# Value products issued two rounds at a time, and causal masks added by half-array matmuls, in an attention loop

## The reference

```python
H, D = 16, 8                                   # 16 heads of 8 columns
q, k, v = heads(x @ Wq + bq), heads(x @ Wk + bk), heads(x @ Wv + bv)
att = where(causal, q @ k.T * D**-0.5, -inf)   # 256 queries, 256 keys
y = softmax(att) @ v
qc, kc, vc = heads(x @ Wcq + bcq), heads(ctx @ Wck + bck), heads(ctx @ Wcv + bcv)
y = y + softmax(qc @ kc.T * D**-0.5) @ vc      # 256 queries, 512 context keys
x = x + tanh(g_xattn[0]) * (y @ Wp + bp)       # x is layer-normalised ahead of the products
```

## Time and profile before

| | us |
|---|---|
| timed runs, median (lowest to highest of 3) | 378.12 (374.95 to 379.81) |
| the profiled execution | 374.34 |
| its span, first to last instruction | 372.6 |
| TensorE busy (share of the span) | 326.8 (88%) |
| VectorE busy | 233.9 (63%) |
| ScalarE busy | 191.7 (51%) |
| mean granted clock of TensorE | 0.948 of full speed |

### The profile page before, as it was taken

The page is one execution under the profiler, slowest core; times in us unless marked ns, Lnnn a source line. Parts: engine busy times, 40 slices in busy tenths (PEclk is TensorE's granted clock), DMA queues, the critical chain, the costliest instruction groups (busy, mean ns, idle before and its releaser), DMA issues.

```text
span 372.6 us, 7109 instructions
## 1 busy us (share of the span) xinstructions
PE 326.8 (88%) x2696; PEld 188.9 (51%) x2696; DVE 233.9 (63%) x546; ACT 191.7 (51%) x397; POOL 110.0 (30%) x202
## 2 busy tenths in 40 slices
PE   4689799979999999789989799999987599899994
PEld 2446433424434344244476467677755266565662
DVE  5889998858888879466442143332213679649765
ACT  3267388858898888557248323322247143323220
POOL 5526231316433233123575003443350201100000
PEclk9999879989999999899989699999998599989999
DMA  7759792960323005230161560000004000000001
GB/s 177 172 124 210 132 195 56 213 187 4 115 74 102 4 2 173 73 102 3 26 214 35 128 184 10 18 23 21 10 21 118 0 0 3 0 0 2 28 1 28
DMA packets 35777, 27.80 MB, mean 75 GB/s; under 512 B 5579, under 2 KB 33022, under 8 KB 35744
## 3 DMA queue, kind: packets, MB, share of 16 engines
q1 hardware_dynamic: 33574, 25.27, 27.4%
q0 software_dynamic: 1280, 1.88, 1.6%
q10 hardware_dynamic: 890, 0.20, 0.3%
HBM read 11.89 MB, written 5.26 MB: 46 GB/s over the span
## 4 chain that ended last, share of the span: by engine, by line
PE 69%; DVE 13%; ACT 6%; DMA 4%; issue 4%; POOL 2%; ACTq 1%; SPq 0%; POOLq 0%; DVEq 0%
PE psum L1468 12%; PE psum L1672 11%; PE psum L1703 7%; PE psum L1691 4%; DVE nmax L1042 4%; PE psum L1434 4%; PE psum L1650 4%; PE psum L1410 3%; PE psum L1486 3%; PE psum L1402 3%; ACT ot_sb L818 2%; PE psum L1412 1%; PE psum L1655 1%; PE psum L1765 1%; PE psum L1437 1%
## 5 line engine op out<-in xcount | busy, mean ns | idle before, releaser
L1042 DVE TENSOR_REDUCE nmax<-psum 128x2 f32<-128x1024 f32 (+2 forms) x88 | 103.2, 1216 | 15.6 <-PE psum L1410 11.3
L843 ACT ACTIVATE parts<-psum 128x512 f32<-128x512 f32 (+1 forms) x88 | 44.7, 569 | 9.3 <-PE psum L1434 8.8
L1672 PE MATMUL psum<-p_more,kcat 128*128 128x320 f32 x128 | 42.6, 475 | 0.7 <-DVE p_more L1176 0.7
L1185 DVE TENSOR_TENSOR qcat<-psum,qk_r 128x320 f32<-128x320 f32 x32 | 15.7, 491 | 42.8 <-ACT qk_r L886 42.6
L733 POOL DMA_INDIRECT rows_back<-qcat,back_at x24 | 22.9, 953 | 53.1 <-ACT qcat L876 48.2
L886 ACT ACTIVATE qk_r<-psum 128x320 f32<-128x320 f32 x32 | 14.0, 437 | 45.2 <-PE psum L1672 45.2
L1703 PE MATMUL psum<-h_t,kcat 128*128 128x512 f32 x64 | 30.9, 608 | 0.7 <-ACT h_t L854 0.7
L1410 PE MATMUL psum<-kcat,qcat 64*128 64x512 bf16 x128 | 25.9, 404 | 5.5 <-DVE nmax L1042 4.8
L1672 PEld LDWEIGHTS psum<-p_more,kcat 128*128 128x128 f32 x128 | 23.4, 200 | 13.5 <-issue 4.6
L1468 PE MATMUL psum<-parts,v_aug 128*9 128x256 f32 (+1 forms) x352 | 28.9, 373 | 0.0
L1434 PE MATMUL psum<-qcat,kcat 64*128 64x256 bf16 x256 | 25.6, 280 | 3.0 <-ACT p_more L843 1.2
(11 more groups left out here) (225 smaller groups left out, 609.5 us busy)
## 6 DMA issues: line engine op xcount, KB each, us to landing
kcat<-parts SPq DMA_DIRECT2D x18, 192.0 KB, 4.1
qcat<-parts SPq DMA_DIRECT2D x24, 128.0 KB, 3.9
kcat<-ones_b SPq DMA_DIRECT2D x8, 192.0 KB, 5.2
kcat<-in_L_ffn_wi_gate_dram SPq DMA_DIRECT2D x6, 256.0 KB, 3.8
kcat<-in_L_ffn_wi_up_dram SPq DMA_DIRECT2D x6, 256.0 KB, 4.0
kcat<-in_L_ffn_wo_dram SPq DMA_DIRECT2D x6, 256.0 KB, 5.5
parts<-in_L_ffn_w_dram SPq DMA_DIRECT2D x3, 512.0 KB, 5.5
rows_in<-zeros SPq DMA_DIRECT2D x1, 1290.0 KB, 5.8
```

Of the source, the lines that this page charges most:

```text
L843: act.activation(p_slots[u % NPT][:, 0:w], s2_bank(s2_place[u])[:, 0:w], ACT.Exp, scale=SCALE).then_inc(p_in, 1)
L1042: dve.tensor_reduce(dst[:, :, n * g:n * (g + 1)], src.rearrange("p (r q k) -> p r q k", r=PAR, q=n), AX.X, ALU.max, negate=True).then_inc( ...
L1185: dve.tensor_tensor(hh[:, e % 2, f, 0:SLOTS], bank(3 + 2 * (i % 2))[:, 0:SLOTS], sg[:, i % 2, 0:SLOTS], ALU.mult).then_inc(hh_in[0], 1)
L1672: ins = pe.matmul(bank(2 + 2 * (i % 2) + m)[:, 0:SLOTS], w_t[e][:, m, f * P:(f + 1) * P], xs_t[:, e % 2, :], start=True, stop=True)
```

## The change

Two things. `ROUNDS_AT` puts rounds 2 and 3 of the values together behind step 3's scores, and rounds 4 and 5 behind step 5's; steps 2 and 4 then have none. And the mask of each tile is added by 64-row matmuls: head `par` 0's by the upper half of the array's rows, head `par` 1's by the lower half, each half in two turns (64 mask rows per turn, shifted by widened tiles `ident_w` and `mask_w`), alternating between the halves. A tile's mask takes two matmuls in place of one. `bv_wide` moves into the space of `got`.

```diff
-        bv_wide = sb("bv_wide", [P, D])
...
-        ident_b = sb("ident_b", [P, P], BF16)
-        mask_b = sb("mask_b", [P, P], BF16)
+        ident_w = sb("ident_w", [P, 2 * P], BF16)
+        mask_w = sb("mask_w", [P, 2 * P], BF16)
+        ident_b = ident_w[:, P // 2:P // 2 + P]
...
         got = sb("got", [P, 2, NT, D])
+        bv_wide = got[:, 0, 0, :]
...
-        ROUNDS_AT = ((), (0, 1), (2,), (3,), (4,), (5,))
+        ROUNDS_AT = ((), (0, 1), (), (2, 3), (), (4, 5))
...
+            link(pool.memset(ident_w[:, :], 0.0))
             const(pool.tensor_copy(ident_b[:, :], ident[:, :]))
-            link(pool.memset(mask_b[:, :], 0.0))
-            const(pool.affine_select(out=mask_b[:, :], in_=mask_b[:, :], pattern=[[-1, P]], compare_op=ALU.is_ge,
-                                     fill=NEG, base=0, channel_multiplier=1))
+            link(pool.memset(mask_w[:, :], 0.0))
+            const(pool.affine_select(out=mask_w[:, :], in_=mask_w[:, :], pattern=[[-1, 2 * P]],
+                                     compare_op=ALU.is_ge, fill=NEG, base=P // 2, channel_multiplier=1))
...
                 if kind != "cross":
-                    for par in range(PAR):
-                        dst, w = bank(first + par), BANK // heads
+                    w = BANK // heads
+                    for turn in range(2):
                         for n in range(heads):
-                            pe.matmul(dst[:, (n + 1) * w - P:(n + 1) * w], ident_b[:, :], mask_b[:, :],
-                                      start=(n == 0), stop=False, skip_group_check=True)
+                            for par in range(PAR):
+                                rows = slice(64 * par, 64 * par + 64)
+                                shift = slice(64 * (1 + par - turn), 64 * (1 + par - turn) + P)
+                                pe.matmul(bank(first + par)[:, (n + 1) * w - P:(n + 1) * w], ident_w[rows, shift],
+                                          mask_w[rows, shift], start=(turn == 0 and n == 0), stop=False,
+                                          skip_group_check=True)
```

## The result

The changed kernel takes 379.75 us (median of 20 runs, 377.5 to 384.47), the kernel before 377.88 in the same series (20 runs, 374.91 to 383.22). The ratio is 1.0049, interval 1.0025 to 1.0072: **slower by 1.9 us** (0.9 to 2.7). The forecast was +4.2 us, a ratio of 1.011. The sign is right and the range holds the time; the size is less than half of the forecast. The kernel before was timed again beside each of three groups of experiments, each on another chip (medians 374.18, 378.13 and 374.13 us); times are compared within a group only.

A forecast was written before the change was run, and what follows sets the result against it. TensorE was taken to bound the kernel, with waits on ScalarE's exps behind each step's scores. Terms 3.32 - 0.64 - 0.47 + 0.66 + 1.32 = +4.2 us on the 378.12 median gave 382.3 us, range 376 to 386.

The forecast's parts named there:

- the wait for the ring: Attention loop: a step's scores wait for the previous step's first exp on ScalarE (three banks); bare, 1.07 or 0.90 us.
- the first gap: TensorE idle 2.36 us at 78.05 for nmax_t copied into qcat; the clock's return there was priced at 0.
- groups 4 to 12: Loop's middle, six steps on four heads each: odd groups +3.32 us, even -0.64, group 12 -0.47.
- groups 13 to 15: Loop's last groups, without maxima: +0.66 us for two longer steps, +1.32 for round 4 coming behind the last step.
- The absorption of groups 1 to 3 in the transfer's wait: Before 78.05 these groups add 1.50 us, hidden in TensorE's 2.36 us wait for a transfer: counted 0.
- rival 1: Attention loop: only TensorE's work counts, the wait on ScalarE having slack; -4.8 us, 373.3; chance 0.10.
- rival 2: Attention loop: new idle makes TensorE's clock fall to 1.2 GHz; 21 us over half the groups, 403; chance 0.05.
- rival 3: Even groups: the 64-row masks don't run in pairs; +3.0 us over five groups, 385.3; chance 0.05.
- rival 4: At 78 and behind the 1.84 gap the clock may not fall, returning up to 1.0 each: 380.3; no separate chance.
- the short gaps: New TensorE idle of some 0.45 us, twice per odd group; the reason given for counting no return of the clock.
- The second gap: Group 12's end: TensorE waits 1.84 us for GpSimd's split of the last maxima; the clock's return was priced at 0.
- the loop's first group: 0: VectorE bounds this group, its maxima running 12.81 us without a gap, so the change adds 0.

The follow-up runs named there:

- experiment 5: Kernel before with part 2's maxima sent to qcat ahead of batch 3's layout in SP's queue: 374.25 against 378.13 us, ratio 0.9902.
- experiment 6: Changed kernel with part 2's maxima sent ahead of batch 3's layout in SP's queue: 379.21 us, ratio 1.0028 to the kernel before.
- experiment 2: Changed kernel with the old ROUNDS_AT, so only the masks are new against the kernel before: 372.33 us, ratio 0.9957.
- experiment 7: Kernel before, unchanged, executed once more for a second trace: 379.83 us.
- experiment 9: Kernel before with 8 unread matmuls ahead of the last turn's wait at 152 us alone: 372.23 us, ratio 0.9958.
- experiment 3: Changed kernel with the doubled rounds behind steps 2 and 4 in place of 3 and 5: 378.66 us, ratio 1.0127 to the kernel before.
- experiment 11: Kernel before with new masks, earlier transfer of part 2's maxima and 8 unread matmuls ahead of the last turn: 369.87 against 378.13 us, ratio 0.9789.
- experiment 10: Changed kernel, unaltered, run again: 375.22 us, ratio 1.0039 to the kernel before.
- experiment 8: Kernel before with 10 unread matmuls ahead of the wait at 78 us alone: 373.1 against 374.13 us, ratio 0.998.
- experiment 4: Kernel before with unread matmuls ahead of both long waits, 10 at 78 us and 8 at 152 us: 370.79 us, ratio 0.9919.

## Why the prediction was right in sign and wrong in size

The stretches of the profiled executions, in us, cut at the loop's first `scores2`, group 4's first, the last `turn`, the last `scores2`, and the experts' first matmul:

| kernel | to group 4 | to last turn | to last scores | to experts |
|---|---|---|---|---|
| before | 32.31 | 74.36 | 25.97 | 31.09 |
| before, once more | 32.96 | 74.57 | 26.16 | 35.55 |
| before, first gap filled | 32.19 | 73.41 | 26.14 | 30.45 |
| before, second filled | 32.17 | 74.39 | 24.68 | 31.21 |
| before, both filled | 32.39 | 73.31 | 24.68 | 31.26 |
| before, early transfer | 31.05 | 73.38 | 24.66 | 35.40 |
| masks alone | 31.58 | 73.11 | 24.65 | 31.32 |
| masks, early transfer, second filled | 29.71 | 71.70 | 24.68 | 34.87 |
| rounds alone | 32.52 | 76.18 | 27.15 | 31.82 |
| pairs behind the other steps | 31.92 | 77.25 | 25.08 | 31.11 |
| after | 31.57 | 75.53 | 27.04 | 33.53 |
| after, once more | 31.63 | 75.56 | 27.24 | 31.36 |
| after, early transfer | 31.74 | 75.56 | 28.31 | 33.68 |

**Right: the wait for the ring, and its size.** Between group 4 and the last turn the change costs 75.55 - 73.36 = +2.2 (two traces each) against the kernel before with its clock kept up behind the first gap; the forecast for groups 4 to 12 was 3.32 - 0.64 - 0.47 = +2.2. From the last turn to the last scores it costs 27.04 - 0.75 (the new fall: 2.00 for 1.25) - 24.68 = +1.6, and the weight transposes behind start another 0.44 later; forecast +1.98 for groups 13 to 15, found 2.0. The absorption of groups 1 to 3 in the transfer's wait is right too, and experiments 5 and 6 show its price when that wait is gone, 1.54.

**Refuted: rivals 1, 2 and 3.** TensorE's work fell by 7 us and the time rose; the middle groups keep 1.00 (but group 15, below, does not); the masks run in pairs.

**Wrong, the step: rival 4, "I take neither, because the short gaps ahead of both remain".** The clock's return behind the two old gaps was a term of the sum, and it was put at nothing. At the first gap the return is 1.0 to 1.3 us, and it came in every trace: with 2.07 to 2.44 of idle there the clock fell in all four traces that have it (before, experiments 2, 7 and 9), with 0.21 to 0.38 in none of three (after, once more, rounds alone), nor with 0.90 in experiment 3. The short gaps of 0.47 ahead of it do nothing that the trace shows. The second gap, worth 1.3 to 1.5 (2.0 in experiment 6, where the lower clock lasted longer), varies from execution to execution: with 1.84 or 1.85 the clock fell in three traces of five (before, once more, first gap filled; not with the masks alone nor in experiment 5), with 1.44 to 1.47 in one of four (in experiment 6; not in after, once more, rounds alone). But experiment 3 has a gap of 2.39 there and no fall, so its length does not decide alone. As means over so few traces (0.60 less 0.25 times 1.4) that is some 0.5 returned, an estimate.

**Wrong, a smaller step: "the loop's first group: 0".** With the new masks the stretch to group 4 is 31.57 to 31.63 (31.92 in experiment 3), with the old ones 32.17 to 32.96: -0.7. The prediction let VectorE bound that group and so gave the masks nothing. Of it 0.2 to 0.3 is seen. The `turn` of part 1, which SP's queue with the transfer for group 4 follows on, starts sooner behind the loop's first scores. How soon also depends on how long the clock, which is low around the loop's start in every trace, stays low behind the first scores (4.3 to 8.5 us). Where that is alike within 0.1 us, the turn starts 9.14 behind the first scores with the new masks and 9.35 with the old (after, before), 9.23 and 9.45 (experiments 2 and 9), 9.60 and 9.92 (experiments 11 and 7). The rest lies within SP's queue and is not explained.

**Missed: a new fall of the clock in group 15**, 0.75 to 0.95, in three traces of five with doubled rounds (after, once more, rounds alone), none of eight with one round per step: some 0.5 lost again, an estimate. That is rival 2's mechanism, at a place where the prediction did not price it.

The sum by these terms: 4.2 - 0.7 - 1.1 - 0.5 + 0.5 = +2.4, measured +1.9 (0.9 to 2.7) and +1.5 (0.3 to 2.7). The terms were read from the traces after the result, so their agreement with it is not a test of them. One timed comparison fits them less well: against the kernel with the first gap filled (experiment 10) the change should cost 4.2 - 0.7 - 0.5 + 0.5 = 3.5 and cost 2.2, with each of the two ratios known to about 0.003, or 1.2 us. So the size of the first gap's return rests on the traces; the timed runs of experiment 8 alone would also allow none. What these runs leave open is how often the clock falls at the second gap and in group 15, since a timed run has no trace; the last half microsecond hangs on that.

## What to carry to other kernels

Moving work away from a place where it covered a wait costs the wait, whatever the move saves: before grouping small blocks to save changes of form, find what each block hides, and price the bare step from a stretch of the same trace that has no such block.

A gap costs its length and, if the clock falls behind it, in these traces between 0.4 and 0.8 times as much again in the next microseconds (1.0 to 1.3 behind 2.07 to 2.44, 1.3 to 1.5 behind 1.84). A change that delays work ahead of such a gap can win that part back, so count it as a term of the sum, and compare traces stretch by stretch, since single stretches vary between executions by as much as such an effect.

## What the runs showed of the hardware

Not expected: the clock is not a function of the gap alone. At the same place of the same loop, 1.84 or 1.85 us of idle brought it to 1.2 GHz in three executions of five and 1.44 to 1.47 in one of four, while 2.39, in the only execution that had it, did not. The Trainium skill ("TensorE: Matmul & The Clock Gate", Part 1) says that the moment at which the clock rises in sustained work varies from run to run of one kernel. The rows here show as much for the fall behind a gap, and that whether it comes at all can vary.

Filling a gap with matmuls that nobody reads, about as long together as the wait, delayed the next scores by nothing that the traces show and bought 0.8% (experiment 4, 0.5% to 1.1%).

The same program's copies on ScalarE behind the loop can come up to 2.3 us late in one execution, with nothing of the kernel to wait for that the profile shows, and on time in another; together such waits moved the experts by some 4 us, twice the effect under study. The long stretch stood in all four traces of one group of runs and in none of the seven of the two others; why is open.
